# Eight blocks of a transformer on one core: square roots moved to a guess and small steps, and the order of every engine rewritten

## The reference

```python
def _layernorm(x, w, b):
    m = jnp.mean(x, axis=-1, keepdims=True)
    v = jnp.mean(jnp.square(x - m), axis=-1, keepdims=True)
    return (x - m) * jax.lax.rsqrt(v + LN_EPS) * w + b
for i in range(6):
    xn = _layernorm(x, ln1_w[i], ln1_b[i])
    q, k, v = heads(xn @ wq[i]), heads(xn @ wk[i]), heads(xn @ wv[i])
    q = softmax(q, axis=-1); k = softmax(k, axis=-2)
    attn = q @ (k.T @ v)
    x = attn @ wo[i] + bo[i] + x
    xn = _layernorm(x, ln2_w[i], ln2_b[i])
    hdn = xn @ w1[i]
    x = where(hdn >= 0, hdn, 0.01 * hdn) @ w2[i] + x
```

## Time and profile before

| | value |
|---|---|
| median of three runs | 1197.98 us |
| profiled execution: span, first to last instruction | 1196.8 us |
| outside of the span, against the median | 1.2 us |
| busy: PE / DVE / ACT / POOL | 1129.7 / 1074.1 / 1035.2 / 1090.7 us |
| DMA queue, share of 16 engines | 56.3% |

### The profile page before, as it was taken

One profiled execution on the slowest core, in us unless ns is written; L12 is line 12 of the kernel. 1 busy time (PEld: TensorE's weight loads), 2 busy tenths in 40 slices (PEclk: granted clock), 3 DMA queues, 4 the chain that ended last, 5 costly groups with the idle time before them and its releaser, 6 DMA issues.

```text
span 1196.8 us, 28581 instructions
## 1 busy us (share of the span) xinstructions
PE 1129.7 (94%) x9722; PEld 864.8 (72%) x9722; DVE 1074.1 (90%) x2885; ACT 1035.2 (86%) x1776; POOL 1090.7 (91%) x920
## 2 busy tenths in 40 slices
PE   7787999999999999999999999999999888999996
PEld 5574687787777777777778778777777755565664
DVE  7889889999999999999999999999987479999973
ACT  5687999999999999999999999999998795767753
POOL 4888999999999999999999999999999888999762
PEclk8799999999999999999999999999999999999998
DMA  8121778768778777687777776866767420110000
GB/s 308 36 71 53 214 213 217 188 209 219 179 205 217 194 216 189 193 221 177 219 212 182 224 202 190 220 194 194 214 188 217 107 61 21 44 37 36 19 19 36
DMA packets 213857, 190.13 MB, mean 159 GB/s; under 512 B 113392, under 2 KB 192080, under 8 KB 213712
## 3 DMA queue, kind: packets, MB, share of 16 engines
q1 hardware_dynamic: 213712, 188.31, 56.3%
HBM read 87.06 MB, written 76.02 MB: 136 GB/s over the span
## 4 chain that ended last, share of the span: by engine, by line
POOL 34%; PE 27%; issue 22%; DVE 10%; ACT 3%; DMA 2%; SPq 2%; DVEq 0%; POOLq 0%; ACTq 0%
POOL hidden L1787 15%; POOL rows_split L1779 6%; POOL arena L1760 4%; POOL arena L1793 3%; PE pair_mlp L576 2%; PE pair_mlp L556 2%; PE ring_pair L615 2%; PE ring_pair L616 2%; PE ring_pair L617 2%; PE pair L567 2%; PE pair L599 2%; DVE ring_pair L1371 2%; DVE arena L1508 2%; PE pair_mlp L674 1%; DVE arena L1389 1%
## 5 line engine op out<-in xcount | busy, mean ns | idle before, releaser
L1787 POOL TENSOR_TENSOR hidden<-hidden 128x2048 f16<-128x2048 f32 x92 | 376.1, 4088 | 0.0
L883 ACT ACTIVATE hidden<-ring_pair,hidden_bias 128x512 f32<-128x512 f32 x384 | 245.6, 686 | 27.9 <-PE ring_pair L617 27.5
L892 ACT ACTIVATE hidden<-hidden 128x2048 f16<-128x2048 f32 x96 | 183.4, 1911 | 17.8 <-PE mlp L633 15.6
L1100 DVE BATCH_NORM_STATS2 bn<-x_all 128x6 f32<-128x128 f32 x896 | 184.2, 278 | 3.2 <-POOL x_all L1739 1.9
L1713 POOL TENSOR_TENSOR rstd<-ve,minus_half 128x8 f32<-128x8 f32 x104 | 170.5, 1640 | 0.0
L852 ACT ACTIVATE arena<-x_all,nmr,rstd 128x128 f32<-128x128 f32 x384 | 157.9, 495 | 0.0
L615 PE MATMUL ring_pair<-arena,halves 128*128 128x512 f16 x384 | 146.1, 381 | 4.5 <-DMA arena<-rows_split 2.8
L616 PE MATMUL ring_pair<-arena,halves 128*128 128x512 f16 x384 | 146.0, 380 | 0.0
L617 PE MATMUL ring_pair<-arena,halves 128*128 128x512 f16 x384 | 145.9, 380 | 0.0
L631 PE MATMUL mlp<-halves,hidden 128*128 128x128 f16 x768 | 135.9, 219 | 1.4 <-POOL hidden L1787 1.4
L633 PE MATMUL pair_mlp<-halves,hidden 128*128 128x128 f16 x768 | 136.5, 220 | 0.0
(11 more groups left out here) (206 smaller groups left out, 3145.1 us busy)
## 6 DMA issues: line engine op xcount, KB each, us to landing
n_away<-all_blocks SPq DMA_DIRECT2D x47, 512.0 KB, 3.3
norm_raw<-n_away SPq DMA_DIRECT2D x188, 128.0 KB, 3.0
k_away<-all_blocks SPq DMA_DIRECT2D x45, 512.0 KB, 2.8
q_away<-all_blocks SPq DMA_DIRECT2D x45, 512.0 KB, 3.3
arena<-k_away SPq DMA_DIRECT2D x180, 128.0 KB, 3.6
arena<-q_away SPq DMA_DIRECT2D x180, 128.0 KB, 3.6
x_all<-in_L_attn_x SPq DMA_DIRECT2D x8, 512.0 KB, 5.4
x_in<-in_L_attn_x SPq DMA_DIRECT2D x8, 512.0 KB, 4.0
```

Of the source, the lines that this page charges most:

```text
L883: act.activation(hidden_t[:, c * W + h * HALF:c * W + (h + 1) * HALF], ring[n % 2], ACT.Prelu, bias=hidden_bias[:, b:b + 1], scale=HIDDEN_ ...
L892: act.activation(half_rows(hidden_hi, h), half_rows(hidden_t, h), ACT.Copy).then_inc(hidden_hi_ready, 1)
L1100: last = nc.vector.bn_stats(bn[:, 6 * t:6 * t + 6], src(t))
L1787: pool.tensor_tensor(half_rows(hidden_lo, h), half_rows(hidden_t, h), half_rows(hidden_hi, h), ALU.subtract).then_inc(hidden_lo_ready, 1)
```

## The change

- `root1` and `root2` become one: the moments of the first norm of item v and of the second norm of item v - 4 stand side by side in `mv12`. ACT guesses the root for both on 128x16 (`root_guess`: Ln, then Exp of -0.5 times it, with a wait between), and POOL improves it by one Newton step: `root_open` (two instructions), `root_square`, `root_scale`, `root_newton`, `root_done`, `root_offset`, all 128x16, each waiting for the one before. No power is left in the 48 items; the eight `front_root` and the sixteen feed-forward roots keep theirs.
- A factor of 128 that the second norm needs now comes with the root, and the first norm's weights are divided by it.
- `keep_warm` and its 172 matmuls are gone.
- ACT loads the table set with both logarithm and exponential at its start. It loads tables twice in the program, as before.
- `product_k` gets a wait on `ctx_o_ready` (item i - 2).
- Every `items(v)` is written in a new order, with other offsets, on PE, ACT, DVE, POOL and SP. The feed-forward phases after it are the same.

```diff
-            def root1(j):
-                pool.tensor_tensor(ve1[:, :], mv[:, :, 1], eps_cols[:, :], ALU.add).then_inc(ve1_ready, 1)
-                root(rstd1, ve1, T, j + 1, pow1_done)
+            def root_guess(v):
+                after(act, mv1_ready, min(v + 1, ITEMS))
+                after(act, mv2_ready, min(v - LAG + 1, ITEMS))
+                after(act, root_steps, rooted(v - 1, SQUARED))
+                act.activation(root_log[:, :], mv[:, :, 1], ACT.Ln, bias=eps_cols[:, 0:1]).then_inc(root_log_ready, 1)
+                act.wait_ge(root_log_ready, v + 1)
+                after(act, root_steps, rooted(v - 1, ROOTED))
+                act.activation(root_y[:, :], root_log[:, :], ACT.Exp, scale=-0.5).then_inc(root_y_ready, 1)
+            def root_open(v):
+                pool.tensor_scalar(root_ve[:, :], mv[:, :, 1], 1.0, LN_EPS, ALU.mult, ALU.add)
+                pool.tensor_scalar(root_shift[:, :], mv[:, :, 0], -1.0, 0.0, ALU.mult, ALU.add).then_inc(root_steps, 1)
+            def root_square(v):
+                pool.wait_ge(root_y_ready, v + 1)
+                pool.tensor_tensor(root_a[:, :], root_y[:, :], root_y[:, :], ALU.mult).then_inc(root_steps, 1)
+            def root_done(v):
+                pool.tensor_tensor(rstd12[v % 2][:, :], root_r[:, :], root_y[:, :], ALU.mult).then_inc(root_steps, 1)
             def product_k(i):
                 pe.wait_ge(norm1_t_ready, i + 1)
+                after(pe, ctx_o_ready, i - 1)
 DVE items(v):
-                if on(v - 2): block_q(v - 2)
+                if 29 <= v < 29 + GATE_STEPS: prepare_gates(v - 29)
+                if on(v - 3): max_k(v - 3)
+                if on(v - 2): block_n(v - 2)
+                if on(v - 4): block_q(v - 4)
```

More of the change, by code:

```diff
@@ L514, in _ @@
             mlp0_bank = mlp[0]
-            filler = identity[:, :].bitcast(F16)
-            def keep_warm(bank, count, semaphore=None, value=0):
-                if semaphore is not None:
-                    pe.wait_ge(semaphore, value)
-                for n in range(count):
-                    nc.tensor.matmul(bank[:, 0:2 * P], filler[:, 0:P], filler, start=True, stop=True)
             def turn_first_n(i):
@@ L787, in items @@
[L787 to L792 removed]
+                if on(v - 3): context_out(v - 3)
+                if v == 53: product_up(0, 1)
+                if on(v - 5): first_mlp(v - 5, 5)
+                if on(v - 6): second_mlp(v - 6, 4)
+                if v == 63: product_gate(2, 1)
+                if on(v - 5): first_mlp(v - 5, 6)
@@ L793, in _ @@
+                if v == 3: turn_first_k(2)
+                if on(v - 2): context(v - 2)
+                if v == 56: product_up(1, 1)
+                if on(v - 4): first_mlp(v - 4, 3)
+                if on(v - 5): second_mlp(v - 5, 3)
+                if v == 2: turn_first_k(1)
+                if on(v - 4): first_mlp(v - 4, 4)
+                if v == 52: product_gate(0, 2)
+            for v in range(ITEMS + 16):
                 items(v)
@@ L1071, in items @@
-                if v == 50: weights_turned()
-            for v in range(ITEMS + 5):
+                if v == 55: x_ties(1)
+                if v == 54: x_square(0)
+                if on(v - 5): exp_q(v - 5)
+                if on(v - 8): hidden_high(v - 8, 0)
+                if v == 59: gate(0, 3)
+                if v == 58: gate(0, 2)
+                if v == 54: x_hat(1)
+                if on(v - 4): first_norm_t(v - 4)
+                if v == 55: gate(0, 0)
+                if v == 7: copy_k(2)
@@ new lines, in items @@
+                if v == 5: front_hat(6)
+                if v == 51: x_epsilon(1)
+                if on(v - 7): copy_hidden(v - 7, 0)
+                if v == 57: x_epsilon(3)
+                if on(v - 7): copy_hidden(v - 7, 1)
+                if on(v - 6): normalise2(v - 6, 0)
+                if on(v - 6): normalise2(v - 6, 1)
+                if v == 56: gate(0, 1)
+                if v == 60: rows_turned(1)
+                if v == 5: prepare_weights(0, range(3, DEPTH))
+                if on(v - 7): copy_hidden(v - 7, 2)
@@ L1074, in _ @@
+                if v == 6: prepare_weights(1, range(3, DEPTH))
+            for v in range(ITEMS + 16):
                 items(v)
@@ L1653, in items @@
[L1653 to L1664 removed]
+                if on(v - 5): bn2_rows(v - 5)
@@ L1665, in _ @@
+                if v == 56: hidden_max(0)
+                if v == 2: front_stats(4)
+                if v == 1: weight_bounds(0)
+                if v == 56: x_lift(2)
+                if v == 54: x_scaled(2)
+                if v == 58: hidden_lift(0, 0)
+                if on(v - 4): add_attention(v - 4)
+                if v == 49: x_rows(1)
+            for v in range(ITEMS + 16):
                 items(v)
```

591 lines of the change are left out of this document (276 added, 315 removed).

## The result

The changed kernel takes 1213.7 us in the median of four runs (1210.2 to 1216.8), the kernel before 1198.0 beside it: a ratio of 1.012, interval 1.0097 to 1.0143. It is slower by 1.2%, and outside of the range 1178 to 1209. Its profiled execution, the slowest of the four, took 1216.8 us with a span of 1215.1, which is 18.3 us more than the span before.

What follows compares the result with a forecast made beforehand. PE and POOL were taken to bound the middle together at 18.3 us per turn. From a span of 1196.8, +1.6 middle, -3.5 start and -2.5 end gave 1192.4, about 1194 us as time, range 1178 to 1209.

Steps and rivals of the forecast that it cites:

- PE and POOL bound the middle at 18.3: Middle turns: PE and POOL both need 18.3 us, so lightening POOL alone can't bring a turn under PE's need.
- the change between f32 and f16: PE, k and q side by side: one such change fewer, 0 to 0.1 us per turn, taken as 0.
- The gate turns: 18 middle turns with a gate step ahead of the maximum of k: 18.7 us instead of 18.4, +5.4 together.
- The circle of q: Loop per item over q's transposition, send, fetch, attend and its sum: 17.8 us, not binding plain turns.
- The start: First items: -5 us from the weight splits and +1.5 from the slower clock, together -3.5.
- weight split -5: Twelve weight splits on DVE at the start: 0 to 6.4 us of being held can come back, taken as 5.
- The cold clock: PE at the start without the unread matmuls: more time at the slow clock, +1.5 us, between 0 and 8.
- The end: After the last k: less PE work before its attend, feed-forward phases unchanged, -2.5 us, between -8 and +3.
- Rival D: Start becomes PE's if its clock stays at 0.50: +8 us there, 1206 us, chance 0.08.
- B: Slower: circle of q 18.2 us in plain turns, 19.4 in gate turns, attend waiting for q: 1206 us, chance 0.22.
- A: Circle of q no bound even in gate turns, all 43 middle turns at 18.26 us: 1180 us, chance 0.18.
- C: No change: ACT or DVE's order holds turns at 18.4, the cold clock eats the start's gain: 1198 us, chance 0.12.

Runs made afterwards that it cites:

- after_again: The changed kernel run once more with nothing altered: ratio 1.0131 to the kernel before, runs from 1210.0 to 1219.8 us.
- experiment 2: Changed kernel with the gate step between second and first moments on DVE, still ahead of the maximum of k: 1205.4 us, ratio 1.0044.
- experiment 12: The best kernel with block_q (transposition of q) one place later on DVE, behind max_q: 1226.1 us, ratio 1.0223.
- the best kernel: Kernel 1 with weight splits moved to where POOL is idle or in small steps, and three feed-forward calls moved earlier: 1194.75 us, ratio 0.9951.
- kernel 1: Changed kernel with the gate steps on DVE moved from ahead of the maximum of k to behind block_q: 1201.7 us, ratio 1.0015.
- experiment 5: Kernel 1 with DVE's weight splits moved to where POOL is idle or in small steps: 1195.1 us, ratio 0.9970.
- 3: Changed kernel with 146 unread matmuls put back on PE in seven places: 1222.5 us, ratio 1.0189.
- 4: The kernel before without its 172 unread matmuls, nothing else changed: 1197.3 us, ratio 0.9981.
- 6: The kernel of experiment 5 with 146 unread matmuls put back on PE: 1208.5 us, ratio 1.008.
- the old roots: Kernel 1 with the old root form, one power on 128x16 and one product on POOL, no Ln and Exp on ACT: 1260.8 us, ratio 1.0495.
- experiment 7: Kernel 1 with three calls of feed-forward unit 1 moved earlier, one on DVE and two on ACT: 1202.7 us, ratio 1.0015.

## Why the prediction was wrong, point by point

The forecast for the span was +1.6 us in the middle, -3.5 at the start and -2.5 at the end. The first profile has +7.7, +3.5 and +7.1, the second (after_again) +11.2, -1.1 and +3.9. So three terms failed. The one of the gate turns is explained by experiments, that of the start in part, and that of the end, which missed by 6.4 to 9.6 us, is not.

**PE and POOL bound the middle at 18.3.** Right that POOL's relief can't bring a turn under PE's need. POOL's share is 79% (forecast 80), its work in a plain turn 15.3 us (15.6), ACT's 17.9 (18.14). But PE's need fell too: q straight behind k starts its successor after 1.78 us where it took 1.84 behind an f16 tile of the second MLP. z and the short product of `context_out` fell by the same 0.06, though they still stand behind f16 work: behind a slice of the first MLP (512 columns) now, behind a tile of the second (128 columns) before. Here is z, before and now:

```profile
610.95 2.00 PE L576 MATMUL pair_mlp<-arena 128*128 128x128 f32 x16
612.79 0.38 PE L615 MATMUL ring_pair<-arena,halves 128*128 128x512 f16 x1
```

```profile
426.70 1.95 PE L579 MATMUL pair_mlp<-arena 128*128 128x128 f32 x16
428.49 0.22 PE L634 MATMUL pair_mlp<-halves,hidden 128*128 128x128 f16 x1
```

So it was not the change between f32 and f16 that I had named and taken as 0 out of 0 to 0.1. Three such places are 0.18, and a plain turn is 0.16 shorter, PE without a gap in both. The stretch of 17 turns without a gate step gave 2.9 us in the first profile, where 2.6 was forecast, but 0.2 in the second, in which six of these turns took 18.6 to 19.3 us (four of 18.5 to 18.8 in the first).

**The gate turns: the step that failed first.** The forecast had them at 18.7 us and +5.4 for all; they are at 18.92 and 19.20, and the stretch cost +12.5 (+12.6 in the second profile). The place was right: a gate step ahead of the maximum of k closes a ring. The price was wrong twice. The ring that binds is the short one over the exponential of k: in all 18 gate turns z starts 0.15 us after that exponential, and in 12 of them attend starts without any wait, 8.37 us later; ahead of the others PE waited 0.3 us at most. And I took the step's 1.25 us from the earlier trace rows as work. It is 0.4 to 0.65 us of work; the rest is waiting for POOL, which in the old place was the end of `hidden_low` and in the new one is `normalise_q`. With 0.65 us the short ring would be 17.7 us by this sum, under PE's 18.10; in experiment 2, at 0.79 us each, the steps in it still cost 3.2 us.

**The circle of q.** My 17.8 us was near: 17.3 in the mean, 18.0 at the longest in the turns of experiment 12 that I counted, with single trips elsewhere up to 0.9 us longer. It is why every later `block_q` costs, and the single turns of 18.3 to 19.3 us that remain in the best kernel fit with it, since its attend waits 17 times there; that these waits are q's transfers was not shown for each.

**The start, forecast -3.5, was +3.5 in the first profile (item 7) and -1.1 in the second.** The term "weight split -5" failed: the twelve took 14.3 and 12.3 us instead of 15.3. And item 0's maximum of k stands 9.1 us later than before (50.7 against 41.6), where I had taken some 5 and that later items catch up; at item 3 it was 5.9 and 1.2 us, so they did, by different amounts. I had read the median of 738 ns as the commoner case and the order as better; three of the new places stood 0.13 us behind POOL's next long instruction (kernel 1):

```profile
109.68 2.36 POOL L1747 TENSOR_TENSOR x_all<-x_all,mod_in 128x1024 f32<-128x1024 f32 x1
109.81 5.52 DVE L1370 SCALAR_TENSOR_TENSOR halves<-hidden,downs,halves 128x512 f16<-128x512 f32 x2
```

Moved by one instruction, and the other six of the same turn right behind the first three, they gave the 6.6 us of experiment 5. The Trainium skill ("SBUF — State Buffer", section "SBUF: two separate sides") has the rule that would have led me there: which of the two engines issues first decides who waits, and for the whole instruction; it names DVE instructions with two inputs in SBUF among those that are held against a GpSimd instruction that reads SBUF. The traces agree: splits, weight and gate steps are held up to 4.5 us, while transposes and sums beside the same POOL instructions keep their 1.2 us. I had cited its lock and not asked who comes first.

**The cold clock, +1.5.** The clock in 80 to 120 us fell from 0.91 to 0.75, as forecast in kind. Rival D's cold start is there in part (it reckoned with 0.50), and no price of it was found: three comparisons with and without fillers (3, 4, 6) all went against the fillers. In the two of the new order a held weight step is part of the loss, so the clock's own price, the 1.5 us, was not measured.

**The end, forecast -2.5, was +7.1, and +3.9 in the second profile** (281.6 us from item 47 on). From an item's maximum of k to its last sum of the MLP it is 91 to 93 us in the middle before and 96 to 102 after, so the pipeline is deeper. A longer drain would be the obvious reading of the loss, but the rows speak against it: the last of these sums, item 47's, starts 88.6 us after its maximum of k before and 72.8 after, and 4.6 us earlier in the program:

```profile
1007.73 0.75 DVE L1261 SCALAR_TENSOR_TENSOR x_all<-mlp,mlp_up,x_all 128x512 f32<-128x512 f32 x1
1003.13 0.75 DVE L1272 SCALAR_TENSOR_TENSOR x_all<-mlp,mlp_up,x_all 128x512 f32<-128x512 f32 x1
```

So the items end earlier, as the forecast of -2.5 had it, and it is the feed-forward units, which I had taken to follow, that come later. Their sixteen powers on POOL (128x4) mark them. Counted from item 47's maximum of k the second stands at 35.4 us before and 40.9 after, the third at 50.0 and 49.0, the fourth at 62.5 and 68.3, and from the seventh on they come every 12.1 us in both kernels (but for one step of 12.4 in the new one), 5.6 to 6.0 us later. The second, before and after, in both right behind a `hidden_low` in POOL's queue:

```profile
954.57 1.03 POOL L1713 TENSOR_TENSOR f_rstd<-f_ve,minus_half 128x4 f32<-128x4 f32 x1
971.17 1.02 POOL L1724 TENSOR_TENSOR f_rstd<-f_ve,minus_half 128x4 f32<-128x4 f32 x1
```

The same lateness shows at the first hidden tile of the fourth unit, 100.6 us after item 47's maximum before and 103.9 to 109.3 in the kernels of the new order (115.8 with the old roots). The clock from 1000 to 1040 us was 0.83 in the first profile and 0.96 in the second. Which step of the first units holds them was not shown; experiment 7 moved three calls of the second unit and ruled those out. This stays open.

The rivals: B had the sign and a time of 1206, with the right stretch and the wrong ring. A and C fell. D gave 1206 too, but by a clock of 0.50 that was not there. Of the signs that I had named, ACT's busy share stayed at 87%, under the 88 that I wanted.

## What to carry to other kernels

A duration in a trace is not a price: where two engines take turns by a lock, look at what the other one started just before, and price the instruction by its shortest case plus what it would meet at the new place. In an order tuned to such gaps, write down the margin in which each held instruction gets in; one of 0.1 us makes the time spread and turns a harmless move into 10%. And list every ring through a moved instruction, also the short ones without transfers.

## What the runs showed of the hardware

- A DVE instruction with two inputs in SBUF, and a TENSOR_SCALAR on f32 there too (L1297, 0.38 us alone), waits for a running POOL instruction to its end: 0.15 to 0.75 us alone, 1.3 to 2.2 behind a 1.94 us one, 3.7 to 4.5 behind one of 4.1. Block transposes, reduces and sums with one input in PSUM kept their 1.2 us beside the same instructions. POOL is held in the same way when DVE is first (0.61 us instead of 0.22, 4.64 instead of 4.09).
- A power on POOL takes 1.01 us on 128x4, 1.64 on 128x8 and 2.90 on 128x16; a product on 128x16 takes 0.22, and Ln and Exp on ACT 0.30 and 0.22.
- Unread matmuls raised the granted clock of the window from 80 to 120 us (0.83 to 0.91, 0.75 to 1.00, 0.87 to 0.96) and made the program slower each time: by 2.7 us in the old order, and by 9 and 13 in the new one, there with a held weight step of 4.5 us as part of it.
- A stage of 16 f32 matmuls of 128 columns takes 1.84 us to the start of its successor behind an f16 matmul of 128 columns, and 1.78 behind an f16 matmul of 512 columns or behind f32.
